# Row maxima with the mask added on VectorE, and attention heads divided after a transfer instead of after transposes

## The reference, cut to what matters

```
k, q, v = proj(W_key), proj(W_query), proj(W_value)      # 16 heads of 16 channels
scores = einsum('bhqd,bhkd->bhqk', q, k) * hd ** -0.5
scores = where(tril, scores, -inf)
weight = softmax(scores, axis=-1)
out = einsum('bhqk,bhkd->bhqd', weight, v)               # then 16 heads side by side: 256 channels
out = einsum('bto,po->btp', out, W_proj) * 256 ** -0.5
```

## Time and profile before

| | |
|---|---|
| runs shown | 1098.3, 5709.19, 1094.94 us; median 1098.3 |
| profiled execution | 1094.69 us, of which span 1092.9 us |
| PE busy | 1016.9 us (93%), 6846 matmuls |
| DVE busy | 501.8 us (46%) |
| ACT busy | 518.9 us (47%) |
| chain that ended last | PE 81%, DVE 7%, issue 3%, ACT 3%, DMA 2% |
| mean granted TensorE clock | 0.976 of full |

### The profile page before, as it was taken

One profiled execution on the slowest core, in us unless ns is written; L12 is line 12 of the kernel. 1 busy time (PEld: TensorE's weight loads), 2 busy tenths in 40 slices (PEclk: granted clock), 3 DMA queues, 4 the chain that ended last, 5 costly groups with the idle time before them and its releaser, 6 DMA issues.

```text
span 1092.9 us, 20884 instructions
## 1 busy us (share of the span) xinstructions
PE 1016.9 (93%) x6846; PEld 701.1 (64%) x6846; DVE 501.8 (46%) x1139; ACT 518.9 (47%) x1379; POOL 192.9 (18%) x184
## 2 busy tenths in 40 slices
PE   3789999999999967989999999999999999999986
PEld 2457777777777754556666666666666656656663
DVE  4522112121121264547457467467467467466451
ACT  2424444444444524256456456456456456454443
POOL 3201001010010052131312312312313213200000
PEclk9889999999999987899999999999999999999999
DMA  6541101011012024435135145245235244224110
GB/s 198 193 136 39 48 29 58 29 39 47 29 58 106 31 86 123 70 98 146 43 131 137 45 137 127 53 135 120 65 133 111 68 140 101 68 73 112 31 40 20
DMA packets 63760, 94.22 MB, mean 86 GB/s; under 512 B 11760, under 2 KB 49136, under 8 KB 63728
## 3 DMA queue, kind: packets, MB, share of 16 engines
q1 hardware_dynamic: 57456, 89.36, 29.0%
q10 hardware_dynamic: 6272, 4.46, 1.3%
HBM read 59.94 MB, written 33.59 MB: 86 GB/s over the span
## 4 chain that ended last, share of the span: by engine, by line
PE 81%; DVE 7%; issue 3%; ACT 3%; DMA 2%; ACTq 1%; SPq 1%; POOL 0%; DVEq 0%; POOLq 0%
PE PS L768 25%; PE PS L972 7%; PE PS L874 6%; PE PS L926 6%; PE PS L907 5%; PE PS L941 5%; PE PS L840 4%; PE PS L755 4%; PE PS L819 3%; PE PS L1003 3%; DVE nm L1622 3%; PE PS L861 2%; PE PS L928 2%; PE PS L943 2%; ACTq L1236 1%
## 5 line engine op out<-in xcount | busy, mean ns | idle before, releaser
L768 PE MATMUL PS<-arena 128*128 128x256 f32 x1024 | 312.1, 421 | 0.0
L1622 DVE TENSOR_REDUCE nm<-PS 128x1 f32<-128x512 f32 (+3 forms) x352 | 207.2, 636 | 89.6 <-PE PS L928 89.5
L1293 ACT ACTIVATE arena<-PS 128x512 f32<-128x512 f32 x256 | 152.2, 600 | 168.2 <-PE PS L943 167.0
L1160 ACT ACTIVATE arena<-PS 64x8 f32<-64x8 f32 x512 | 88.5, 173 | 184.4 <-PE PS L755 180.7
L755 PEld LDWEIGHTS PS<-arena 128*72 128x72 f32 x1024 | 129.9, 141 | 68.1 <-ACT arena L1160 4.6
L768 PEld LDWEIGHTS PS<-arena 128*128 128x128 f32 x1024 | 155.5, 192 | 0.0
L941 PE MATMUL PS<-Q,K 98*128 98x512 bf16 (+3 forms) x512 | 130.9, 301 | 7.6 <-ACT arena L1293 5.6
L1478 DVE SCALAR_TENSOR_TENSOR arena<-arena 128x512 f32<-128x512 f32 x16 | 11.1, 694 | 265.7 <-ACT arena L1171 265.7
L926 PE MATMUL PS<-K,Q 96*128 96x256 bf16 (+3 forms) x512 | 121.1, 304 | 4.4 <-DMA K<-qk_d 2.5
L755 PE MATMUL PS<-arena 128*72 128x8 f32 x1024 | 121.3, 191 | 0.0
L928 PE MATMUL PS<-negmask,identb 128*128 128x128 bf16 x512 | 96.2, 222 | 0.0
(11 more groups left out here) (172 smaller groups left out, 1324.3 us busy)
## 6 DMA issues: line engine op xcount, KB each, us to landing
qk_d<-QB SPq DMA_DIRECT2D x24, 512.0 KB, 3.0
X<-in_L_attn_x SPq DMA_DIRECT2D x12, 512.0 KB, 3.5
Q<-qk_d SPq DMA_DIRECT2D x32, 192.0 KB, 4.0
K<-qk_d SPq DMA_DIRECT2D x32, 192.0 KB, 4.3
arena<-xt_d SPq DMA_DIRECT2D x16, 256.0 KB, 3.2
gt_d<-arena SPq DMA_DIRECT2D x16, 256.0 KB, 2.5
wx_d<-arena SPq DMA_DIRECT2D x16, 256.0 KB, 2.0
XT<-xt_d SPq DMA_DIRECT2D x8, 512.0 KB, 4.5
```

The source lines that it names most:

```text
L768: mm = pe.matmul(o, lhs, rhs, start=first, stop=last)
L1293: s_.activation(PR[:, g % 2, j, at:at + T], PS[:, bank, :], ACT.Exp, scale=SCORE_SCALE).then_inc(t_e.sem, 1)
L1622: v_.tensor_reduce(nm[:, g, h:h + n, i], PS[:, u % 3, 0:n * (i + 1) * P].rearrange("p (n w) -> p n w", n=n), AX.X, ALU.max, negate=True).t ...
```

## The change

`scores` makes no mask matmul. `rowmask` (128 x 512, zero except the last 128 columns) is added by VectorE's `tensor_tensor_reduce`, one per head, which writes back into PSUM and gives the maximum; a memset ahead of it takes the wait. The sign is now turned in `maxima_high` and `maxima_low`. VA is all ones outside the channels, so that rows 16 to 31 of a head's 32 all hold the sum. The transposes, `take_heads` and their semaphores go. SyncE copies OS to AO (channels) and DEN (16 equal rows of sums) with eight transfers per group; VectorE divides once per two groups, 128 x 512 at a time: after `maxima(8)` of stage 2 (groups 0 and 1) and after `maxima(10)` of the next sequence's stage 0 (groups 2 and 3).

```
-        negmask = sb("negmask", [P, P], BF16)
+        rowmask = sb("rowmask", [P, T], BF16)
+        begun = sb("begun", [P, SU])
-        AT = sb("AT", [P, NT, D])
-        rec = sb("rec", [P, NT, NT])
+        AO = sb("AO", [P, KT, T])
-        AO = QF[:, 0:KT, :]
+        DEN = (HM, QF[:, 2, :])
...
+            def load_heads(b, g): 
+                sp.wait_ge(o_e.sem, o_e.at(b, g + 1))
+                k, at = g // 2, g % 2 * GH * HD
+                for h in range(GH):
+                    to = slice(at + h * HD, at + (h + 1) * HD)
+                    sp.dma_start(AO[to, k, :], OS[32 * h:32 * h + HD, :]).then_inc(o_ld.sem, 16)
+                    sp.dma_start(DEN[k][to, :], OS[32 * h + HD:32 * h + 2 * HD, :]).then_inc(o_ld.sem, 16)
...
             def stage0(b, more, first=False):
                 if not first:
+                    load_heads(b - 1, 3)
                     load_x1(b - 1, more)
...
             def stage1(b, more, more2):
+                load_heads(b, 0)
                 if more2:
                     load_rows(b + 2)
                     load_gates(b + 2)
...
                     save_operands(b + 1, 2)
+                load_heads(b, 1)
+                if more:
                     load_operands(b + 1, 0, True)
...
             def stage3(b, more):
                 if more:
                     load_operands(b + 1, 2, True)
+                load_heads(b, 2)
...
-            g_.memset(VA[:, :, :, :], 0.0).then_inc(f_set, 1)
-            pool.wait_ge(f_set, 1)
-            g_.memset(VA[:, :, :, HD:HD + 1], 1.0).then_inc(f_set, 1)
+            g_.memset(VA[:, :, :, :], 1.0).then_inc(f_set, 1)
...
                 for e in range(n):
-                    pe.matmul(PS[:, bank, e * w:(e + 1) * w], Q6[0:KS, g * GH + h + e, i * P:(i + 1) * P],
-                              K6[0:KS, g * GH + h + e, 0:w], start=True, stop=False)
-                    mm = pe.matmul(PS[:, bank, (e + 1) * w - P:(e + 1) * w], identb[:, :], negmask[:, :],
-                                   start=False, stop=True)
+                    mm = pe.matmul(PS[:, bank, e * w:(e + 1) * w], Q6[0:KS, g * GH + h + e, i * P:(i + 1) * P],
+                                   K6[0:KS, g * GH + h + e, 0:w], start=True, stop=True)
...
-            def values_turn(b, g):
...
-            def heads_turn(b, more):
...
-            def take_heads(b, ahead=1):
...
-            def project(b, n):
+            def project(b, n, more):
                 if n == 0:
-                    pe.wait_ge(r_e.sem, r_e.at(b, KT))
+                    pe.wait_ge(o_v.sem, o_v.at(b, KT))
+                if more:
+                    pe.wait_ge(s_v.sem, s_v.at(b + 2, n + 1))
...
             def take_values(b, g):
                 act.wait_ge(o_mm.sem, o_mm.at(b, g + 1))
-                act.wait_ge(o_t.sem, o_t.at(b, g))
+                act.wait_ge(o_ld.sem, o_ld.at(b, 2 * GH * g))
...
             def maxima(b, g, u):
-                v_.tensor_reduce(nm[:, g, h:h + n, i],
-                                 PS[:, u % 3, 0:n * (i + 1) * P].rearrange("p (n w) -> p n w", n=n), AX.X, ALU.max,
-                                 negate=True).then_inc(m_r.sem, 1)
+                v_.memset(begun[:, u:u + 1], 0.0)
+                w = (i + 1) * P
+                for e in range(n):
+                    most = v_.tensor_tensor_reduce(out=PS[:, u % 3, e * w:(e + 1) * w], in0=PS[:, u % 3, e * w:(e + 1) * w],
+                                                   in1=rowmask[:, T - w:], scale=1.0, scalar=-BIG, op0=ALU.add,
+                                                   op1=ALU.max, accum_out=nm[:, g, h + e, i:i + 1])
+                most.then_inc(m_r.sem, 1)
...
-            def divide(b, g):
+            def divide(b, k):
+                dve.wait_ge(o_ld.sem, o_ld.at(b, H * (k + 1)))
+                v_.reciprocal(DEN[k], DEN[k]).then_inc(o_r.sem, 1)
+                dve.wait_ge(o_r.sem, o_r.at(b, k + 1))
+                v_.tensor_tensor(AO[:, k, :], AO[:, k, :], DEN[k], ALU.mult).then_inc(o_v.sem, 1)
...
-                    side = {6: [], 7: [lambda: divide(b - 1, 3)]}
+                    side = {10: [lambda: divide(b - 1, 1)]}
...
-                side = {6: [lambda: divide(b, 1)]}
+                side = {8: [lambda: divide(b, 0)]}
```

More of the change, by code:

```diff
@@ L297, in two_layers @@
         o_mm = count("o_mm", G, 2)
[L298 to L303, removed]
+        o_e = count("o_e", G)
+        o_ld = dcount("o_ld", 2 * H)
+        o_r = count("o_r", KT)
+        o_v = count("o_v", KT)
         z_mm = count("z_mm", 2, 3)
@@ L533, in _ @@
             g_.memset(ident[:, :], 0.0).then_inc(const, 1)
-            g_.memset(negmask[:, :], 0.0).then_inc(const, 1)
+            g_.memset(rowmask[:, :], 0.0).then_inc(const, 1)
             g_.memset(negmask_t[:, :], 0.0).then_inc(const, 1)
@@ L546, in _ @@
                              pattern=[[-1, P]], channel_multiplier=1).then_inc(const, 1)
-            g_.affine_select(out=negmask[:, :], in_=negmask[:, :], compare_op=ALU.is_ge, fill=-BIG, base=0,
+            g_.affine_select(out=rowmask[:, T - P:], in_=rowmask[:, T - P:], compare_op=ALU.is_ge, fill=-BIG, base=0,
                              pattern=[[-1, P]], channel_multiplier=1).then_inc(const, 1)
@@ L975, in values @@
                 mm.then_inc(o_mm.sem, 1)
-            def values_turn(b, g):
[L979 to L982, removed]
-            def heads_turn(b, more):
[L986 to L995, removed]
-            def project(b, n):
-                if n == 0:
-                    pe.wait_ge(r_e.sem, r_e.at(b, KT))
+            def project(b, n, more):
+                if n == 0:
+                    pe.wait_ge(o_v.sem, o_v.at(b, KT))
+                if more:
+                    pe.wait_ge(s_v.sem, s_v.at(b + 2, n + 1))
+                elif more is not None:
+                    pe.wait_ge(w_e.sem, w_e.at(b + 1, NT))
                 for j in (2 * n, 2 * n + 1):
@@ L1035, in stage0 @@
                         side[2].append(lambda: leave(b + 1, 1))
-                    side[2].append(lambda: values_turn(b - 1, 3))
-                    side[4].append(lambda: heads_turn(b - 1, more))
-                    side[6].append(lambda: project(b - 1, 0))
-                    side[7].append(lambda: project(b - 1, 1))
+                    side[6].append(lambda: project(b - 1, 0, more))
+                    side[7].append(lambda: project(b - 1, 1, more))
                 side[8].append(lambda: value(b, 0, first))
@@ L1044, in stage1 @@
             def stage1(b, more):
-                side = {0: [lambda: values(b, 0)], 2: [lambda: values_turn(b, 0)]}
+                side = {0: [lambda: values(b, 0)]}
                 if more:
-                    side[2].append(lambda: normal_turn(b + 1))
+                    side[2] = [lambda: normal_turn(b + 1)]
                     for n, k in enumerate((3, 4, 6, 7)):
@@ L1053, in stage2 @@
             def stage2(b, more):
-                side = {0: [lambda: values(b, 1)], 2: [lambda: values_turn(b, 1)]}
+                side = {0: [lambda: values(b, 1)]}
                 for n in range(8):
@@ L1059, in stage3 @@
             def stage3(b, more, more2):
-                side = {0: [lambda: values(b, 2)], 2: [lambda: values_turn(b, 2)]}
+                side = {0: [lambda: values(b, 2)]}
                 if more2:
                     side[1] = [lambda: mix(b + 2, 0, True)]
-                    side[2].append(lambda: mix(b + 2, 1, True))
+                    side[2] = [lambda: mix(b + 2, 1, True)]
                 if more:
@@ L1116, in _ @@
             values(B - 1, 3)
-            values_turn(B - 1, 3)
-            heads_turn(B - 1, None)
-            project(B - 1, 0)
-            project(B - 1, 1)
+            project(B - 1, 0, None)
+            project(B - 1, 1, None)
         @block.scalar
@@ L1125, in _ @@
             s_ = nc.scalar
-            for s in (a_xt, c_h, c_t, g_t, n_x2, n_xt, q_e, q_1, d_e, h_e, e_t, t_e, o_e, r_e, x_n, a_ue, g_h, m_a, n_xn,
+            for s in (a_xt, c_h, c_t, g_t, n_x2, n_xt, q_e, q_1, d_e, h_e, e_t, t_e, o_e, x_n, a_ue, g_h, m_a, n_xn,
                       w_e):
@@ L1297, in take_values @@
                 act.wait_ge(o_mm.sem, o_mm.at(b, g + 1))
-                act.wait_ge(o_t.sem, o_t.at(b, g))
+                act.wait_ge(o_ld.sem, o_ld.at(b, 2 * GH * g))
                 s_.copy(OS[:, :], PS[:, 5, :]).then_inc(o_e.sem, 1)
-            def take_heads(b, ahead=1):
-                act.wait_ge(q_2.sem, q_2.at(b + ahead, 2))
-                for k in range(KT):
-                    act.wait_ge(r_t.sem, r_t.at(b, k + 1))
-                    s_.copy(AO[:, k], PS[:, 6 + k, :]).then_inc(r_e.sem, 1)
             def store(b):
@@ L1329, in stage0 @@
                     side[1] = [lambda: take_values(b - 1, 3)]
-                    side[4] = [lambda: take_heads(b - 1)]
                 stage(b, 0, side)
@@ L1685, in stage1 @@
             def stage1(b, more, first=False):
```

(8 more changed lines are left out.)

27 lines of the change are left out of this document (9 added, 18 removed).

## The result

| | before | after |
|---|---|---|
| median, us | 1097.25 | 1219.14 (1215.08 to 1222.2) |
| ratio to before | | 1.109, interval 1.106 to 1.112 |
| profiled span, us | 1092.9 | 1220.4 |
| PE busy / matmuls | 93% / 6846 | 85% / 6142 |
| DVE busy | 46% | 49% |

The kernel is 10.9% slower. Slower was forecast, but with +77 us; it is +122 (medians), and 1219 lies above the range, whose end was 1205.

What follows compares the result with a forecast made beforehand. TensorE was taken as the bound on average (93% busy). From the profiled 1094.7 us, stage gains and losses and the end's +6.4 made +33, 1128; the clock added 44, giving 1172 us, range 1118 to 1205.

Steps and rivals of the forecast that it cites:

- The reciprocal: VectorE's division: 3.2 us for 512 elements per partition, by the slope between rows of 4 and 16; bounds 0.6 and 8.0.
- both stands of TensorE: TensorE idle 4.0 us before `maxima_turn` in stage 2; in stage 0, 1.4 before `maxima_turn` and 3.8 before `project`.
- a sign of being wrong: Listed signs: reciprocal near 0.7 us, a maximum with a second instruction, or no TensorE idle stretch above 2.5 us.
- The step that failed: SyncE's queue in stage 1: heads' transfers delay loads for b + 2 by 5 us, harmless because used a stage later.
- The clock: Half clock behind new TensorE stalls in layer 1: 3.2 us per stage 0, 2.5 per stage 2, 1.9 at the end; 44 us.
- Stage 2: Sums' landing, `divide` and late maxima delay the next stage by 3.4 us; 24.1 us long with the clock term.
- The end: Last OS to `project`: 9.8 us instead of 3.3, costing +6.4, and `project` at half clock +1.9.
- A: Rival: the clock holds, because stalls are shorter or fall otherwise; 1128 us, chance 0.20.
- B: Rival: the reciprocal runs at other operations' rate, 0.65 us; 1087 us, no change that can be told, chance 0.12.
- C: Rival: faster, TensorE's whole saving arrives as stage 2's low parts come early enough; 1049 us, chance 0.08.
- D: Rival: reciprocal or maxima dearer; 1214 us with a reciprocal of 6 us, 1190 by the skill's eight cycles; chance 0.08.
- TensorE's saving: 512 mask matmuls save 28.7 us, transposes 14.1 + 7.0 us; in all 49.8 us.

Runs made afterwards that it cites:

- run 11: Changed kernel with four transfers per group, stage 1's loads ahead of them, no reciprocal and VectorE's loop written out: 1133.82 us, ratio 1.030.
- run 6: Changed kernel with stage 1's loads for b + 2 issued ahead of the eight heads' transfers: 1194.49 us, ratio 1.085.
- Run 5: Changed kernel with unused fp32 products on TensorE, 9 ahead of the maxima's turn in stage 2 and 7 ahead of `project`: 1189.95 us, ratio 1.080.
- run 7: Changed kernel with four heads' transfers of 32 partitions per group instead of eight of 16, output not right: 1165.34 us, ratio 1.060.
- run 12: Changed kernel with VectorE's loop over the middle sequences written out and nothing else: 1216.47 us, ratio 1.106.
- run 15: Changed kernel, all values right, with loads first, 9 and 7 unused TensorE products and VectorE's loop written out: 1171.61 us, ratio 1.064.
- Run 9: Kernel before with the masked maxima alone (heads divided through transposes) and VectorE's loop written out: 1091.91 us, ratio 0.994.
- run 16: Kernel before with VectorE's loop written out and nothing else: 1099.0 us, ratio 1.000.

## Why the prediction was right in sign and wrong in size

**What held.** The reciprocal, 3.35 us against 3.2: the slope between two short rows of the same operation carried to 512 elements within 5%. The Trainium skill's repeat count of 8 (VectorE: DVE Perf Modes, "First, the fixed hardware budget"), read as cycles per element, had given an estimate of 4.4. Issue 0.63 us apart (0.6), landing 2.0 (1.8), the place and length of both stands of TensorE, stage 3 (21.2 against 20.9), stage 0 (26.2 to 26.8 against 27.3). A maximum has a second instruction, which I had listed as a sign of being wrong; but the starts of 512-wide ones in a row are 0.65 us apart (0.66 forecast for a unit), since the read and the next add overlap. From run 11:

```profile
670.86 0.73 DVE L1606 CUSTOM_DVE_ANT_0 PS<-PS,rowmask 128x512 f32<-128x512 f32 x1
...
671.52 0.72 DVE L1606 CUSTOM_DVE_ANT_0 PS<-PS,rowmask 128x512 f32<-128x512 f32 x1
```

**The step that failed:** "In stage 1 they hold the loads for b + 2 back by 5 us; these are used a stage later." I asked when the loads' data is *needed* and costed them at nothing. What counts is what they now *collide with*. They are issued 7.5 us later (from 2.8 to 10.3 us after `values`), and they are still landing when the maxima rows are sent at 686.7. The landing of the second maxima transfer, which the next stage waits for, shows what that does. Times in us; "issued" is counted from the stage's `values`:

| kernel, sequence | issued | to landing | stage 1 |
|---|---|---|---|
| before, b = 1 | 14.6 | 1.8 | 19.7 |
| after, b = 1 | 14.3 | 5.9 | 22.2 |
| after, b = 2 to 5 | 15.4 to 15.5 | 4.8 to 5.6 | 21.9 to 23.1 |
| after, b = 6 (no loads) | 14.2 | 1.8 | 19.1 |
| run 6, b = 1 | 14.3 | 1.8 | 19.2 |
| run 6, b = 2 to 5 | 15.4 to 15.6 | 1.8 | 20.3 to 20.5 |

So a transfer of 4 KB landed 3 to 4 us late behind the loads. In b = 1 that makes 3.0 us (22.2 against run 6's 19.2) of the 3.7 by which stage 1 missed its forecast of 18.5: TensorE's wait, and the half clock behind it. Run 6, which moves only the order in the queue, gives 25 us back, half of the 50 us by which the profiled execution lies above the forecast. It also mends the second collision, GpSimd's addition on VectorE's subtractions. No run has the one without the other, but the trace leaves little room for the second: in the sequence shown in the split above, TensorE already stood for the maxima rows (594.4 to 596.35) when the slow subtraction began at 595.64, and in stage 2 VectorE then stands 2.4 us for the sums in any case, more than the 1.3 to 2.1 us that the two subtractions of a sequence lose.

**The clock.** The forecast charged 22.4 us in stage 0, 20 in stage 2 and 1.9 at the end. Run 5 gave 29 us back, with 30 of 123 us at half clock left in stages 2 and 0. In proportion the whole would be 39 us; that is my estimate from these numbers. So the 44 are neither confirmed nor refuted.

**Stage 2** was 1.0 to 1.5 us too short. It starts at half clock behind stage 1's wait (1.98 us in the sequence shown), so OS is copied 1.2 us later in the stage than forecast, and the chain from there to the turn of the maxima took 12.3 us instead of 11.5; TensorE's work behind it took 6.8 instead of 7.8. Run 6 shows that most of the excess is stage 1's error passed on: an edit in stage 1's queue alone shortens stage 2 by 9.3 us in all, of an excess of 11.7.

**The end:** OS to `project` 10.5 us (forecast 9.8), `project` at half clock 6.73 us for 16 products against 3.72 in the earlier trace rows:

```profile
1197.07 0.58 ACT L1289 COPY OS<-PS 128x512 f32<-128x512 f32 x1 [2.48 <-PE PS L982]
...
1208.13 6.73 PE L997 MATMUL PS<-w_pr,AO 128*128 128x256 f32 x16 [11.12 <-DVE AO L1622]
```

That is 1.8 us more than forecast, ahead of the last output. The forecast had put +1.9 us for half clock on a `project` of 3.72, where twice the time would be +3.7; +3.0 came.

**The sum.** Stage by stage against the forecast with its clock terms, over the eight sequences, the changed kernel is longer by 27.0 us in stage 1, 11.7 in stage 2, 4.9 in stage 3 and 0.4 in stage 0: 44 us. With 1.8 at the end and 4.2 ahead of the first `values` that makes the 50 us by which the profiled 1222.2 lies above 1172; the part ahead of `values` differs by as much between kernels that are alike there (first `values` at 476.3 us here, 473.2 in run 7, 476.7 in run 6).

Of stage 1's 27.0 us, the order in the queue makes 15.2 (run 6). VectorE's stand makes some 3: stage 1 falls by 2.9 us in all with the loop written out (run 12), and by 3.2 between runs 6 and 15. The other 9 stay even where both are mended (run 15): stage 1 takes 19.2 us and not 18.5, so less than half of TensorE's saving comes, and 20.4 in b = 0 and 15.1 in b = 7, where 18.4 and 12.7 were forecast.

Two small slips in the prediction change nothing: by the unit prices given, the masked maxima cost VectorE 1.06 us more per stage and not 1.2; and one idle stretch of TensorE in layer 1 of the kernel before, at 470.8, was 2.18 us long and not under 2, and the granted clock did not fall behind it.

**The rivals.** A (the clock holds), B (the reciprocal at an ordinary rate) and C (faster) did not come. D came near the time by luck, 1214: neither reciprocal nor maxima were dearer.

**TensorE's saving** of 49.8 us. Run 9 takes the mask matmuls' 28.7 us alone and shows 6.8. A steady sequence takes 79.8 us instead of 81.2: 1.4 of the 3.6 us possible. TensorE's waits on VectorE's longer maxima, 9.1 and 6.3 us in all against 1.3 and 1.1 before, take up more than half of the rest, and stage 1 is longer than before at both ends (20.8 instead of 19.6 in b = 0, where run 16 also has 21.3, and 15.7 instead of 13.9 in b = 7). In the maxima-only kernel as first written, even this is lost to the four stands of VectorE.

**What stays open:** of run 11's 35 us, how much is the way through OS itself and how much the half clock in stage 2; and the full price of the half clock. Nor did I follow stage 3's 4.9 us, 2.4 of which are in the first sequence.

## What to carry to other kernels

When a transfer is put ahead of others in a queue, don't stop at when the data of those others is needed: write down when they will land and what else runs then, on the queues and on the engine that they release. Count transfers, not bytes, when the chain through them is on the path. And when a change makes an engine's loop longer, look for a stand at the loop's turn before judging the change; one line (the loop written out) turned the masked maxima from no gain into a small one.

## What the runs showed of the hardware that I had not expected

**A loop's turn can cost 2.3 to 2.6 us on VectorE.** It appears when the masked maxima lengthen the body (q14: 39 packets against 15; VectorE's rows in one sequence 240 against 117), not with the kernel before, and goes when the loop is written out (26 packets). By the Trainium skill, Runtime: NRT & Kernel Launch, section "Instruction fetch mechanics", an engine's instruction memory is two pages, prefetched in sequence, and a taken branch to outside of them waits for a fetch. The runs agree: four stands at the loop's four turns, of 2.3 to 2.6 us each.

**An issue of the heads' transfers costs 0.59 us, from 16 partitions (32 KB) or from 32 (64 KB)**, and lands 2.0 us later in both cases. It isn't the same for every transfer: the loads XT and WX, 512 KB each, were issued in 0.35 and 0.38 us.

**A small transfer behind large ones lands late.** The 4 KB of maxima rows, sent from ScalarE's queue 2 to 4 us after the last of SyncE's three loads, took 4.8 to 5.9 us to land instead of 1.8.

**GpSimd's additions held up VectorE's operations on two SBUF tiles:** the subtraction 1.90 instead of 1.22 us on average, the multiply 2.33 instead of 0.69 beside a 2.34 us addition, while the reciprocal, of one input, took its usual 3.35 us beside the addition at 655.16. The Trainium skill, SBUF — State Buffer, section "SBUF: two separate sides", calls the shared port pair an exclusive lock for the length of an instruction; the multiply's 2.33 us fits that.
